# Another order of the lead-up pieces on all five engines of a four-layer kernel

## The reference

```python
x = L0(x, cond_2048, mask0)   # linear attention, 16 heads of 16, FiLM, projection
x = L1(x, cond_2048, mask1)   # softmax attention, 16 heads of 16, FiLM, projection
x = L2(x, cond_2048)          # two selective scans (one backwards), E=512, N=16, gated
x = L3(x, cond_2048, mask2)   # linear attention, 8 heads of 32, FiLM, projection
# each attention layer, in short:
q, k, v = norm(x) @ Wq, norm(x) @ Wk, norm(x) @ Wv
y = attention(q, k, v)
x = x + silu(norm(y) * (1 + scale) + shift) @ Wo     # scale, shift from silu(cond) @ W
# each scan of L2, over time t, for 512 channels e and 16 states n:
h[e, n] = exp(delta[t, e] * A[e, n]) * h[e, n] + delta[t, e] * B[t, n] * u[t, e]
y[t, e] = sum_n C[t, n] * h[e, n]
```

## Time and profile before

| | us |
|---|---|
| median of three runs | 4864.47 |
| lowest, highest run | 4858.75, 4867.07 |
| profiled execution, its own time | 4873.8 |
| its span | 4872.1 |
| first instruction of strand W on TensorE | 91.6 |
| first drive product of the scans (GpSimd, L763) | 442.0 |
| end of the last drive product | 4811.7 |

### The profile page before, as it was taken

The page is one execution under the profiler, slowest core; times in us unless marked ns, Lnnn a source line. Parts: engine busy times, 40 slices in busy tenths (PEclk is TensorE's granted clock), DMA queues, the critical chain, the costliest instruction groups (busy, mean ns, idle before and its releaser), DMA issues. The chain is left out here.

```text
span 4872.1 us, 73002 instructions
## 1 busy us (share of the span) xinstructions
PE 3984.9 (82%) x25940; PEld 2580.9 (53%) x25940; DVE 4130.2 (85%) x5616; ACT 3652.0 (75%) x8614; POOL 4015.4 (82%) x1900
## 2 busy tenths in 40 slices
PE   4767788888888888888888888888888888888655
PEld 3544455555555555555555555555555555555433
DVE  4313888998999998999999989999999899999885
ACT  0135778887888887888888888888888888888764
POOL 0003888998999998999999989999999899999995
PEclk7767798998999998999999999999999899999876
DMA  4002434443444434444444334444444344444441
GB/s 116 3 4 70 100 80 99 104 105 89 110 105 111 98 85 99 104 107 95 107 105 113 96 84 104 102 105 97 106 107 111 91 90 103 101 107 95 106 109 36
DMA packets 321177, 458.00 MB, mean 94 GB/s; under 512 B 55450, under 2 KB 148741, under 8 KB 320809
## 3 DMA queue, kind: packets, MB, share of 16 engines
q1 hardware_dynamic: 320810, 453.32, 39.8%
HBM read 374.51 MB, written 78.17 MB: 93 GB/s over the span
## 5 line engine op out<-in xcount | busy, mean ns | idle before, releaser
L763 POOL TENSOR_TENSOR S_X<-S_slot,S_bc 128x1024 f32<-128x1024 f32 x1024 | 2398.5, 2359 | 137.4 <-PE ps L798 125.5
L704 ACT ACTIVATE ps<-S_slot,acol 128x256 f32<-128x256 f32 x4096 | 1721.6, 465 | 203.5 <-DVE S_X L734 130.6
L719 DVE TENSOR_TENSOR_SCAN ps<-ps,S_X 128x512 f32<-128x512 f32 x1088 | 1299.2, 1212 | 38.2 <-ACT ps L704 25.4
L719 DVE TENSOR_TENSOR_SCAN S_X<-ps,S_X 128x512 f32<-128x512 f32 x960 | 1151.5, 1208 | 71.1 <-ACT ps L704 69.0
L776 POOL TENSOR_TENSOR S_X<-S_X,S_bc 128x1024 f32<-128x1024 f32 x480 | 1134.1, 2366 | 52.4 <-DVE S_X L719 52.4
L734 DVE TENSOR_TENSOR S_X<-ps,S_bc 128x512 f32<-128x512 f32 x1088 | 718.6, 680 | 9.0
L798 PE MATMUL ps<-S_X,sum 128*32 128x256 f32 x8192 | 649.0, 415 | 84.9 <-POOL S_X L776 84.2
L430 DVE TENSOR_REDUCE A_sm<-ps 128x4 f32<-128x1024 f32 x256 | 313.8, 1226 | 218.5 <-PE ps L373 215.1
L798 PEld LDWEIGHTS ps<-S_X,sum 128*32 128x32 f32 x8192 | 198.7, 113 | 365.2 <-issue 194.7
L373 PE MATMUL ps<-A_kP,A_qP 32*128 32x256 f32 x2048 | 338.9, 454 | 51.3 <-DVE A_sm L430 50.0
L392 PE MATMUL ps<-A_qP,A_kP 32*128 32x256 f32 x2048 | 309.1, 421 | 57.8 <-ACT A_ring L469 36.1
(11 more groups left out here) (293 smaller groups left out, 7234.4 us busy)
## 6 DMA issues: line engine op xcount, KB each, us to landing
S_slot<-scr_dd SPq DMA_DIRECT2D x1024, 256.0 KB, 4.6
scr_dd<-C_dd SPq DMA_DIRECT2D x64, 1024.0 KB, 6.5
S_bc<-scr_bc SPq DMA_DIRECT2D x256, 256.0 KB, 5.3
C_mod<-scr_mod SPq DMA_DIRECT2D x32, 384.0 KB, 7.4
L_xin<-in_x SPq DMA_DIRECT2D x32, 256.0 KB
out_x<-xs SPq DMA_DIRECT2D x32, 256.0 KB, 3.1
T_gate<-scr_mod SPq DMA_DIRECT2D x32, 128.0 KB
S_X<-in_L_cond_Wc SPq DMA_DIRECT2D x2, 1024.0 KB, 6.9
```

The costliest lines, as they stand in the source:

```text
L704: ins = a.activation(B["bank"][half_at(b, u, i)][:, n * T:(n + 1) * T], B["slot"][:, s, j, 0, :], ACT.Exp, scale=K.k["acol"][:, s, LINES * ...
L719: v.tensor_tensor_scan(line(x if u in ON_POOL else decay), line(decay), line(x), 0.0, ALU.mult, ALU.add).then_inc(S.scan.sem, 1)
L763: g.tensor_tensor(B["X"][:, u % RING], B["slot"][:, s, :, 1, :], rep(B["bc"][:, s, q, :], 1, LINES), ALU.mult).then_inc(S.b.sem, 1)
```

## The change

Only the table FIRST is replaced, for all five engines. Each string keeps its length and the count of every letter; TURN and all pieces stay. So every engine does the same pieces, each strand in its old order, and only the interleaving of strands differs.

```diff
--- before.py
+++ after.py
@@ -1481,18 +1481,18 @@
 
 FIRST = {
     "PE": (
-        "WWWWWWWWWWWWWWWLLLLWLWWWWWLWWLWWWWWWWWWWWWWLWWWWWWLWWWWWWWWWWWWWLAAAAAAAAAAAAAAAAAAAAAAAAAAALLLLALLLLLLAAAAAACACAACACACA"
-        "ACAAAAACAAAAACACAACACLLLCLALLLLLCLSASAAAAASCACSAACACACASACSAASSSASAASCAASAASACASSCSASSACSASSSSCLSLLSCLSSASSLSLLSSLLSCSSL"
-        "STSAS"),
+        "WWWWWWWWWWWWLLWLLWWWWWLWWWWLWLWWWWWWWWWWWWLWWWWWWWLWWWLWWWAWAAAAAWWAAAWAWAAWAAAAAWAAAAAALAAALLALLLLLLALAAAAAAAACACACACAA"
+        "CACAAAACAAAACAACALACCALLLALLLCLLCSSLSAAAACAAACACACASSACAACASASSASAACASASACAASSSSSAACACSSSLASSLSLSSCSSLALCLSLSSLSSSLCSSSL"
+        "SSTSA"),
     "DVE": (
-        "WWWWLWWWWWWWWWWWWWWWLWLWWWWLWLWWWWWWWWWWWWWWWWWLWWWWWWWWWWWWWWLWLWWWWWWWWWWWWWWWWWWWWWWWLWAWWWAAAAAAAAAAAAALLLLLALLLLACA"
-        "CAAAAAAAAACAAALLLLLALCLLSSPPLSACSSPSSPSACSASPPASASASPASAPASSASPASPSGSSPSPCSSSSPPSSSPSSPSSSPSPSSASPAGPSASSSPPSLSSSPPSSLLS"
-        "SPPSLSSLSPPSGSSAPSSPLCLLSS"),
+        "WWWWWWWWWLWWWWWWWWLWWLWWWWWLWWWWLWWWWWWWWWWWWWWWWWLWWWWWWWWLWWWWWWLWWWWWLWAWWWWAAWWAWAWAWALWAAWAWAWAAALLLLWWLWWLLAWCLACW"
+        "AAALAAAAAAACAAASLLPLLSCASPCLLLSSSLAPPCSASSPASSASPASPASASAPASASAPSPSSCSPSPSGSSPSPSSLSPSPSSSPSPSSSPAASSPGSASSPPSSSSPPSLLSS"
+        "PSLPSLSSPSSPSGSSSLAPPLLSCS"),
     "ACT": (
-        "LLLWLLLLLLLLLLAAAAAAAAAAAAAAAAAALALALALLLLLLLLLLAACAACACCCCCCCCACAAAAAAACACAACCAALALCCACLALLLLLCCLLLLLSCSCCSCSSSASACSASS"
-        "ACASCCSSSCSSCSCSCCCASSCSASSASASSASASSASSASCACSSASSASSSCSSSCASSSSALSALSSCCASSCLASSLSSLSSSLSLLCSCSSLSSL"),
-    "Pool": "LALCCCCCACSLSSCSPCCSSSSSCPSPSSCPSSSPCSPSPSSSPSSPSSPSSSSPPSASPSPCSP",
-    "SP": "LAWWALACCACCLsAsCCssSCSASCSCLStSsAsCCssSCSA",
+        "LLLLLLWLLLLLLLAAAAAAALAAAAAAALAAALLAALLLALALLLLLCAACAAACLCCCCCACCCAAAACAAAACSACACACLCACSSALAALCLLLLSSCLLLLLSCSCCCAACASCA"
+        "SCSSSACSCSCSSCSSCCSACSSCSSAASSASSASSACSASASSASSACSSCASSLSSSASSASSLSCSSAASSLSALSSSLLSCSSLCLSCCSLSSCLSS"),
+    "Pool": "LALCCCCCSASCSLPCCCSSSPCSSSSPSPSSPCCSPSSPSSSPSSSSSPPSSSPASPSSPPSSPC",
+    "SP": "LWAWCLAALACCssCCtAssLCSSACCSSSSsACsCCssSCSA",
 }
 
 TURN = {
```

## The result

The changed kernel took 4820.41 us in the median of four runs (4813.69 to 4829.73), the kernel before in the same series 4865.77: ratio 0.991, 95% interval 0.9886 to 0.9933. In a later series it was 0.9906 (0.9879 to 0.9933). The execution profiled first took 4813.69 us with a span of 4812.0, a second one 4833.44 with 4831.5; the one of before 4873.8 with 4872.1.

What follows compares the result with a forecast made beforehand. VectorE and GpSimd bound the turns, a one-batch latency chain the lead-up. 10.9 - 1.4 us at A0, 12 kept to C1.m1, plus 2, gave 14 off the 4864.47 median: 4850, range 4833 to 4867.

Steps and rivals of the forecast that it cites:

- (b): Before batch 1: VectorE's full queue swallows the gain; 4862 us, chance 0.22 together with the edit doing nothing.
- (c): Repeated turns: their changed phase brings more long turns, some 3.6 us each; slower, 4876 us, chance 0.11.
- Step 1: L0's output product moves ahead of ten W pieces: L0 ends 11.65 us sooner, A0's statistics start 10.9 sooner.
- Step 2: Ten W products between A0's products cost 1.4 us; A0's last transposes end at 265 instead of 274.5.
- rival (a): TensorE's clock rises in A0 and batch 0's stalls go: gain 28 us, 4836, chance 0.17.
- Step 3: L1 pulled into A0's gaps: L1's last step 18.5 us sooner, A0's last step only 2 sooner.
- Steps 4 and 6: C0 keeps 13.8 of 24 us; L2's end comes 12.3 us sooner, C1.m1 12.8.
- Step 5: First scan product on GpSimd near 377 for 442, 65 us sooner, none of it counted as gain.
- Step 7: Batch 0 up to the first turn: 2 us counted of GpSimd's longest wait of 6.8 for TensorE's sums.

Runs made afterwards that it cites:

- e3: Changed kernel with the last ten W pieces and their evictions put back ahead of L0's output step; 4835.43 us, ratio 0.9941 to the kernel before.
- e13: Changed kernel plus unread identity transposes on TensorE in A1 and L1, none in A0; 4812.65 us, ratio 0.9876 to the kernel before.
- e10: Changed kernel plus unread identity transposes on TensorE in A0, A1 and L1; 4823.05 us, ratio 0.9896 to the kernel before.
- e11: Changed kernel plus unread identity transposes on TensorE in A0 and L1 only; 4833.35 us, ratio 0.9914 to the kernel before.
- e9: Changed kernel with A1, C0, L2, batch 0's scan units 0 to 3 and their DMAs in the old order; 4830.03 us, ratio 0.9914.
- e6: Changed kernel with twelve unread GpSimd operations, about 8 us, added ahead of C0.du0; 4825.16 us, ratio 0.9905 to the kernel before.
- e8: Changed kernel with the first scan product and its VectorE steps put back behind A1, ScalarE's exponentials left moved; 4827.61 us, ratio 0.9916.
- e2: Kernel before with only W, L0, A0, L1 and VectorE's first C0 statistics in the new order; 4833.55 us, ratio 0.9938.
- e5: Changed kernel with the tail of batch 0 (A2, C1, scan units from 4 on) in the old order; 4825.49 us, ratio 0.9914.

## Why the forecast was wrong, step by step

**Bounds and direction: right.** The gain is mostly that S1.0 comes sooner, and the turn's work is the same. Neither (b) nor (c) came true: nothing was swallowed, and S1.0 to the last product took 4203 and 4220 us for 4214. By the table of four parts the miss up to S3.0 is 36.8 us: 15.7 in steps 1 to 3, which I took at their old durations, leaving out the clock, 6.3 in steps 4 to 6, where the mechanism was wrong, 6.6 behind L2.x and 8.2 in the first turns, which I had at nothing.

**Step 1, mis-sized.** L0.x came 15.1 us sooner and not 11.65 (A0's statistics 14.7 and not 10.9). The re-ordering gave what I worked out; the rest is the clock: L0.o to L0.x took 2.2 us where it took 4.2 (170.0 to 172.2, and 183.1 to 187.3), its first four matmuls are 1.03 us for 2.05, the two levels of the clock, and W's pieces ahead of it were 1.4 to 1.9 us sooner.

**Step 2, the price right, the clock left out.** I charged 1.4 us for W's products between the scores. The first score step to the maxima's transposes took 26.9 us (27.8 in the second profile), against 26.3 before and 25.3 in e3, where W stands ahead: 0.6 to 2.5, so that price holds. But A0's last transposes came 18.3 us sooner and not 9.5. A0's projections now follow L0 and W without a gap: from the start of q0 to that of v they took 7.9 us for 10.7 (9.9 in e3), and the clock of 89 to 189 was 0.89 for 0.79. From the maxima's transposes to the last ones it was 39.2 us for 41.1. That is rival (a) in part of its mechanism only: A0's later score steps still took 3.4 to 4.0 us each, and its 4836 is 16 above the result. Two of my readings behind rival (a) were off. A granted clock of 0.79 means the lower level for some 42 of the 100 us (an estimate: full is 1, the lower level a half), not for most of them. And the 2.46 us that I took for a score step of A1 was the shortest; A1's eight maxima, 344.7 to 367.5, are 3.3 a step. By the Trainium skill ("TensorE: Matmul & The Clock Gate", Part 1: The HAM clock gate) the halved clock is the default and recent activity releases it; e13's rows agree with it. Those of A0 do so only in part: from 189 to 290 TensorE was busy 83.3 of the 101 us in e10 and 88.7 in e11, and the clock was 0.72 and 0.66, against 0.63 and 0.61 in the changed kernel's two profiles and 0.66 in e13, which has nothing added in A0.

**Step 3, right but for the clock.** L1.q started right behind the last transposes, L1.q to hT took 25.6 us for my 30.2, with A0's hT inside and its output product behind, as said. A0.x came at 286.2, 16.4 us sooner for 2, and L1.x at 289.4, 34.2 sooner for 18.5. Of the 16 us missing, 9 were there at L1.q. The rest is L1 itself, 33.4 us from L1.q to L1.x for my 39.8 (38.5 before): its first four matmuls are 1.03 us for 2.07.

**Steps 4 and 6, the mechanism that failed.** I let A1 and L2 pay for what the new order puts among their pieces: of 18.5 us at L1.x 14.5 were left at A1.h and 12.3 at L2.x, so L1.x to L2.x was to take 6.2 us more. It took 129.7 for 129.7. C0 did give back the 10 us that I had written (C0.st to C0.dbc0 is 30.3 us for 20.4), and A1 did pay: from L1.x to its reciprocal it took 91.5 us (90.6 in the second profile), for 86.8 before and 87.6 in e9, which has the middle old. What I had at nothing is a gain behind it. From A1's reciprocal to A1.x it took 17.6 us for 22.6 (22.6 in e9 too), and from A1.x to L2.x 20.5 for 20.3, where I had charged 2. The stretches from A1's last maximum to its reciprocal and from there to A1.x, before and then in the changed kernel (columns as in the earlier trace rows):

```profile
367.52:410.44 42.92, 30.45 (x155) 17.08 (x156) 2.46 (x3) 14.32 (x19) 2.44 (x2) 0.60 0.21 57
410.44:433.03 22.59, 16.87 (x70) 12.48 (x71) 5.12 (x15) 14.13 (x35) 1.27 (x1) 0.85 0.00 1
```
```profile
334.60:380.91 46.31, 35.24 (x167) 20.39 (x168) 2.45 (x3) 16.22 (x23) 4.79 (x3) 0.57 0.30 70
380.91:398.53 17.62, 12.30 (x58) 8.90 (x59) 9.36 (x14) 14.38 (x33) 4.19 (x3) 1.00 0.00 1
```

In the first stretch TensorE has 4.8 us more work, among it a product of C0 of 3.1 us that now stands ahead of the transposed maxima. In the second the granted clock is 1.00 for 0.85, and ScalarE no longer has L2's normalisation between A1's steps. Its last operation, before and changed:

```profile
418.10 1.09 ACT L153 ACTIVATE T_xh<-L_xin,T_nb,T_rs 128x256 f32<-128x256 f32 x2
```
```profile
314.14 1.09 ACT L153 ACTIVATE T_xh<-L_xin,T_nb,T_rs 128x256 f32<-128x256 f32 x2
```

So the 129.7 for 129.7 is two changes of 4 to 5 us that cancel. I had counted what that normalisation costs C0 (2.3 us) and not what A1 gains by it. Which part of the 5 us is ScalarE's order and which the clock's, no run separates. By e6 the GpSimd part of C0, 8 us late, holds up neither A1 nor L2. And C1.m1 did not wait for C_mod, as I had written, but for ScalarE's normalisation of C1, 4.2 us of idle in its row.

**Step 5, nearly right in what it says, blind in what it leaves out.** S0.0 sooner is worth little, some 3 us by e8. It came at 361.9 and not at 377, and C0.du1 at 397.9 and not at 417.5, again without a gain to match. But the exponentials moved along with it, and I counted only their cost in A1, and not that ScalarE is rid of them behind L2.x (2.0 us at C1's normalisation and at C1.m1, counted from L2.x, changed kernel against e2).

**Step 7, too small.** I counted 2 of the 6.8 us of the longest wait, because VectorE waits for A2's scores there in any case. By e5 the tail is worth 5, and by e9 the middle another 3.5 behind C1.m1; against the kernel before the two have 6.4 there (125.5 us for 131.9).

**The turns: not seen.** I took the number of long turns to be chance and the first two to be like any. In every profile with middle and tail both old they are 281 us, in the others 269 to 273. What makes TensorE's clock fall to 0.79 in the first turn, though both kernels run the same order there, I could not settle: with either half of the new order it did not. Nor is it shown how often a long turn comes later: three and nine in two executions of one kernel, both outside the six give or take two that I had named. The middle's 3.5 us behind C1.m1 I did not take apart either.

## What to carry to other kernels

Where in-order engines run two chains side by side, find out which of them has slack before passing a delay from one to the other: a delay of known size put into each chain in turn costs one run apiece. It answers for the engine that it is put on, and not for the time that the chain's pieces take on the others. And where a piece is moved ahead, count what it costs there and also what it frees at its old place. For a ladder of moments from a profile, take differences between neighbouring pieces rather than the moments: the tail's 5 us (e5) were plain in L2.x to S1.0 and invisible at S1.0. And a forecast for a latency chain should price each step at both clocks, since filling the idle of TensorE can pay twice: at A0's end here 18 us, where the moved work at old durations was worth 9.5.

## What I had not expected of the hardware

Work that computes nothing made this kernel faster: 110 added transposes on TensorE in A1 and L1, and 14.5 us less, in one series. Two executions of the same instructions can stand 6 us apart after 290 us of span (e10 and e11), while the 134 us from L2.x to S1.0 repeat to 0.8 us in ten profiles. A long turn takes 4 us more than the others, and one program had three in one execution and nine in the next, 17 us of spread with no change in the code.
